# A four-layer graph network on one core: input rows loaded by ScalarE's queue, index rows turned amid the table, and shares of the node stages given to GpSimd

## The chip, the cores and the metric

One Trainium2 chip, one core. The time is the device time of one execution in microseconds (us), as a median of three runs. PE is TensorE, DVE is VectorE, ACT is ScalarE, POOL is GpSimd, SP is SyncE.

## The reference

Four graph layers over the same graph of 6250 nodes with 128 features and 100000 edges, sorted by destination. Each layer takes h = relu(layernorm(x)) and adds its result to x:

```python
h = relu(layernorm(x)); x = x + gat(h)      # 8 heads, softmax over the edges of a node and its own loop, batch norm
h = relu(layernorm(x)); x = x + gcn(h)      # sum over edges, scaled by the roots of both degrees, a product, batch norm
h = relu(layernorm(x)); x = x + pna(h)      # mean, deviation, minimum and maximum over edges, 13 parts times W, batch norm
h = relu(layernorm(x)); x = x + gatv2(h)    # leaky relu of x_l[src] + x_r[dst], a dot product, softmax, weighted sum
```

The GATv2 layer ends with `relu(out / denominator + bias)`, which is added to x and stored.

## The kernel before

The nodes stand in 49 tiles of 128 rows; `X` holds all of x in SBUF (128 partitions x 49 tiles x 128). The edges stand in 832 steps of 128, eight steps to a group, 104 groups. The program is a chain of blocks; between two blocks all engines meet. There are ten of them:

1. `build_steps`: loads x and the weights, counts how many edge chunks belong to each step, gathers the edges of each step from DRAM, makes index rows from them, and at the same time makes the first node table (layer norm, a transpose, a product with W: `rows_of`, `turn_rows`, `project`).
2. `gat_pass`, names beginning with `e_`.
3. `gat_to_gcn`, names `f0_` and `r0_` (printed `f_` and `r_`).
4. `sum_pass`, `s_`. 5. `gcn_to_pna`. 6. `moments_pass`, `m_`.
7. `pna_to_gatv2`, names `f2_` and `r2_` (printed `f_` and `r_`).
8. `gatv2_pass`, `v_`, and the end of `layer_gatv2`.

A pass (`gat_pass`, `sum_pass`, `moments_pass`, `gatv2_pass`) begins with POOL gathering the source rows of one step at a time from the node table in DRAM by an indirect DMA (`gather_step`, line 856, or L1749), into a ring of group buffers `G`. The other engines turn each group into sums per destination tile, which DVE adds into `ACC`. Before the first addition `ACC` is set to zero, once per pass.

A node stage (`gat_to_gcn`, `gcn_to_pna`, `pna_to_gatv2`) goes over the 49 tiles in chunks of four (13 chunks) or, in `pna_to_gatv2`, of three (17 chunks). Its second half is written with the class `ResidualNorm`, whose steps for chunk j are: `apply` (ACT, batch norm and relu on columns), `back` (PE, transposes back to rows), `add` (DVE, X += result), `statistics` (DVE, mean and variance of each row), `row_root` (POOL, 1/sqrt as a power), `shift` (DVE, nmr = -mean/deviation), `normalise` (ACT, H = relu(X*rstd + nmr)), `turn` (PE), `turned_in` (ACT copy from PSUM to `HT`), and a product on PE. In `pna_to_gatv2` the order of PE in round j is `back(j)`, `turn(j - 2)`, product(j - 3), and both bias rows are added by DVE when it takes the products out of PSUM (L2616 and L2618).

The order of the work on every engine is that of the written loops: nothing is reordered by a scheduler. Waits are counts of semaphores. In `build_steps`, PE first counts chunks (L616, L620), then turns and projects the table chunk by chunk (L628, L635), and turns the index rows at its end (L658); DVE takes those out of PSUM (L602 to L606). The last block's end is short:

```python
for t in range(tl.start, tl.stop):
    ins = V.scalar_tensor_tensor(ACC[:, t, 1:D + 1], ACC[:, t, 1:D + 1], rd[:, t:t + 1], g["bias3"][:], ALU.mult, ALU.add)
...
V.scalar_tensor_tensor(g["X"][:, tl, :], ACC[:, tl, 1:D + 1], 0.0, g["X"][:, tl, :], ALU.max, ALU.add)
```

## Time and profile before

| | us |
|---|---|
| median of 3 runs | 4756.52 (4754.43 to 4757.53) |
| the profiled execution | 4756.6 |
| its span in the profile | 4754.8 |
| `build_steps` | 0 to 82.3 |
| `gat_pass` | 82.3 to 1165.4 |
| `gat_to_gcn` | 1165.8 to 1259 |
| `sum_pass` | 1259 to 2250 |
| `gcn_to_pna` | 2250 to 2329 |
| `moments_pass` | 2329 to 3390 |
| `pna_to_gatv2` | 3390 to 3643.6 |
| `gatv2_pass` | 3643.6 to 4728.5 |
| the rest of `layer_gatv2` | 4728.5 to 4754.8 |

The times of the stages are read off the timeline: a stage begins with the first instruction of its block. The profile shows one execution; it names for each instruction the idle time of its engine ahead of it and what ended that time. Since each block waits for the one before it, a stage that is shortened by a microsecond shortens the whole by one, unless its last engine is held by something else.

### The profile page before, as it was taken

The numbers are of one execution on the slowest core, as the hardware profiler recorded it, in microseconds if no ns is written. First come the engines' busy times: TensorE is split into PE (matmuls) and PEld (weight loads), VectorE is DVE, ScalarE is ACT, GpSimd is POOL, SyncE is SP. The second block draws the span as 40 slices with busy tenths as digits, with TensorE's granted clock in tenths as the row PEclk, the third lists the DMA queues.
The fourth block names the chain that finished last, engine by engine and source line by source line (L and its number), as shares of the span: only waits on it lengthen the run. The fifth ranks groups of instructions, "written<-read, shape, count | busy, mean of one in ns | idle before, by whom it ended". The sixth has DMA issues, their size and how long they took to land. (4 is left out here: it accounts for less than half of the span.)

```text
span 4754.8 us, 95466 instructions
## 1 busy us (share of the span) xinstructions
PE 3336.3 (70%) x21401; PEld 2878.0 (61%) x21402; DVE 3192.4 (67%) x8183; ACT 2417.6 (51%) x5426; POOL 3323.1 (70%) x3505
## 2 busy tenths in 40 slices
PE   3888888887533333334577777777696888888886
PEld 2666666666533333333476676767564777777775
DVE  5888888888533333334677777787656676666767
ACT  3666666665300000000577777777535666666664
POOL 4777777775677777776677777777524777777774
PEclk7555555555755566655799999899897888888887
DMA  7333333332122121111366666666422333333332
GB/s 131 88 84 86 86 84 86 86 86 54 49 52 53 53 53 53 53 53 44 120 184 184 185 185 185 181 186 183 145 63 50 76 79 80 80 80 80 79 78 72
DMA packets 367220, 462.19 MB, mean 97 GB/s; under 512 B 104067, under 2 KB 271235, under 8 KB 367104
## 3 DMA queue, kind: packets, MB, share of 16 engines
q0 software_dynamic: 107648, 226.35, 20.4%
q1 hardware_dynamic: 254176, 233.02, 16.3%
q10 hardware_dynamic: 5280, 1.58, 0.1%
q8 instruction: 36, 0.59, 0.1%
q14 instruction: 80, 0.66, 0.0%
HBM read 327.40 MB, written 134.06 MB: 97 GB/s over the span
## 5 line engine op out<-in xcount | busy, mean ns | idle before, releaser
L856 POOL DMA_INDIRECT e_G<-dr_tab,src_idx x832 | 810.3, 974 | 266.6 <-issue 253.2
L856 POOL DMA_INDIRECT m_G<-dr_tab,src_idx x832 | 798.2, 959 | 262.7 <-issue 246.4
L856 POOL DMA_INDIRECT v_G<-dr_tab,src_idx x832 | 791.5, 951 | 264.5 <-issue 248.3
L1749 POOL DMA_INDIRECT s_G<-dr_tab,chunk_src x784 | 740.0, 944 | 241.9 <-issue 238.6
L1837 PE MATMUL s_OUT<-s_G,s_S 128*128 x1664 | 380.2, 421 | 586.1 <-SPq L1781 578.4
L1837 PEld LDWEIGHTS s_OUT<-s_G,s_S 128*128 128x128 f32 x1664 | 354.7, 324 | 611.4 <-issue 611.4
L1793 DVE TENSOR_TENSOR ACC<-ACC,s_OUT 128x129 f32 x832 | 241.3, 290 | 604.5 <-PE s_OUT L1837 500.8
L1261 PE MATMUL e_OUT<-e_RH,e_S 128*128 128x144 f32 x1664 | 512.4, 476 | 2.4 <-DVE e_RH L1147 2.4
L2277 ACT COPY f_AT<-r_TP 128x512 f32<-128x512 f32 (+1 forms) x13 | 7.2, 555 | 973.6 <-PE r_TP L2299 973.6
L1994 DVE TENSOR_TENSOR ACC<-ACC,m_OUT 128x256 f32 x832 | 347.3, 417 | 222.3 <-PE m_OUT L2077 126.2
L1261 PEld LDWEIGHTS e_OUT<-e_RH,e_S 128*128 128x128 f32 x1664 | 405.3, 327 | 35.8 <-DVE e_RH L1147 18.4
L2076 PE MATMUL m_OUT<-m_G,m_S 128*128 128x128 f32 x1664 | 344.5, 290 | 41.2 <-DVE ACC L1994 39.1
L1567 DVE SCALAR_TENSOR_TENSOR ACC<-ACC,v_R,v_OUT 128x129 f32 x832 | 287.2, 345 | 83.3 <-issue 0.8
L2077 PE MATMUL m_OUT<-m_SQ,m_S 128*128 128x128 f32 x1664 | 332.1, 282 | 0.0
L1957 ACT COPY m_XB<-m_BK 128x512 f32<-128x512 f32 x416 | 226.8, 587 | 204.6 <-PE m_BK L2060 201.6
L1658 PE MATMUL v_OUT<-v_RH,v_S 128*128 128x129 f32 x1664 | 311.1, 343 | 0.8 <-DVE ACC L1567 0.8
L1173 DVE TENSOR_TENSOR ACC<-ACC,e_OUT 128x144 f32 x832 | 252.8, 304 | 83.4 <-PE e_OUT L1261 0.4
L2051 PE MATMUL m_GT<-eye,m_G 128*128 128x128 f32 x832 | 133.4, 312 | 249.1 <-DMA m_G<-dr_tab,src_idx 196.5
L2076 PEld LDWEIGHTS m_OUT<-m_G,m_S 128*128 128x128 f32 x1664 | 265.4, 201 | 65.3 <-DVE ACC L1994 58.4
L1447 ACT COPY v_NXS<-v_NX 128x512 f32<-128x512 f32 x208 | 120.4, 579 | 310.9 <-PE v_NX L1611 304.2
L1658 PEld LDWEIGHTS v_OUT<-v_RH,v_S 128*128 128x128 f32 x1664 | 264.6, 241 | 18.2 <-ACT v_RH L1462 10.8
L1021 ACT ACTIVATE e_APART<-iota_row,e_LOC 128x128 bf16<-128x128 f32 x832 | 264.1, 388 | 19.4 <-ACT e_LOC L1017 19.1
(380 smaller groups left out, 8123.9 us busy)
## 6 DMA issues: line engine op xcount, KB each, us to landing
dr_ends<-m_XB SPq DMA_DIRECT2D x416, 256.0 KB, 3.2
e_LR<-dr_row_loc SPq DMA_DIRECT2D x104, 256.0 KB
m_MS<-dr_row_start SPq DMA_DIRECT2D x104, 256.0 KB
v_LR<-dr_row_loc SPq DMA_DIRECT2D x104, 256.0 KB
e_G<-dr_tab,src_idx POOLq DMA_INDIRECT x832
m_G<-dr_tab,src_idx POOLq DMA_INDIRECT x832
v_G<-dr_tab,src_idx POOLq DMA_INDIRECT x832
s_G<-dr_tab,chunk_src POOLq DMA_INDIRECT x784, 2.5
```

The lines of the kernel that those rows point to most:

```text
L856: pool.indirect_dma_start(out=out, out_offset=None, in_=table, in_offset=bass.IndirectOffsetOnAxis(ap=g["src_idx"][:, step:step + 1], axis ...
L1021: ins = nc.scalar.activation(APART[:, s, :], g["iota_row"][:], ACT.Square, bias=LOC[:, b, s:s + 1], scale=-1.0)
L1173: V.tensor_tensor(dst, dst, OUT[:, s // 3, (s % 3) * AC:(s % 3 + 1) * AC], ALU.add).then_inc(acc_done, 1)
L1261: nc.tensor.matmul(OUT[:, s // 3, (s % 3) * AC:(s % 3 + 1) * AC], S[:, b % 2, s, :], RH[:, b % 2, s, :], start=True, stop=True).then_inc(m ...
L1567: V.scalar_tensor_tensor(dst, dst, R[:, b % 2, s:s + 1], OUT[:, s // 3, (s % 3) * AC:(s % 3 + 1) * AC], ALU.mult, ALU.add).then_inc(acc_do ...
L1658: nc.tensor.matmul(OUT[:, s // 3, (s % 3) * AC:(s % 3 + 1) * AC], S[:, b % 2, s, :], RH[:, s, :], start=True, stop=True).then_inc(mm_done, 1)
L1749: pool.indirect_dma_start(out=G[:, c % (RING * GROUP), 0:D], out_offset=None, in_=table[:, :], in_offset=bass.IndirectOffsetOnAxis(ap=g["c ...
L1793: V.tensor_tensor(dst, dst, OUT[:, b, s // PER, (s % PER) * AC:(s % PER + 1) * AC], ALU.add).then_inc(acc_done, 1)
L1837: ins = nc.tensor.matmul(OUT[:, b, s // PER, (s % PER) * AC:(s % PER + 1) * AC], S[:, b, s, :], G[:, bass.ds(slot, 1), :].rearrange("p o c ...
L1994: V.tensor_tensor(dst, dst, OUT[:, q % 3, (s % 2) * 2 * D:(s % 2 + 1) * 2 * D], ALU.add).then_inc(acc_done, 1)
L2076: nc.tensor.matmul(OUT[:, q % 3, lo:lo + D], S[:, c, s, :], G[:, b, s, :], start=True, stop=True)
L2077: ins = nc.tensor.matmul(OUT[:, q % 3, lo + D:lo + 2 * D], S[:, c, s, :], SQ[:, c, s, :], start=True, stop=True)
```

## The change

In `build_steps`, the loads of x leave SP's queue and stand in ACT's queue, ahead of the nineteen weight loads. POOL's roots of the first four sets of rows stand ahead of the gathers of the edges. DVE's statistics of the first rows stand earlier. PE counts the chunks after the first product instead of at the start, and turns edges, locations and chunk numbers during the table (rounds 10 to 13); at the end only the `loc_end` rows are turned.

```diff
+                for i in range(EARLY):
+                    root(i)
...
-                whole_tiles = (TILES - 1) * P
-                rows = x[0:whole_tiles, :].rearrange("(t p) d -> p t d", p=P)
-                for c in range(4):
-                    piece = slice(c * XCN * CN, (c + 1) * XCN * CN)
-                    sp.dma_start(g["X"][:, piece, :], rows[:, piece, :]).then_inc(x_in[c], 16)
-                sp.dma_start(g["X"][0:LAST, TILES - 1, :], x[whole_tiles:N, :]).then_inc(x_in[4], 16)
...
+                whole_tiles = (TILES - 1) * P
+                rows = x[0:whole_tiles, :].rearrange("(t p) d -> p t d", p=P)
+                for c in range(4):
+                    piece = slice(c * XCN * CN, (c + 1) * XCN * CN)
+                    act.dma_start(g["X"][:, piece, :], rows[:, piece, :]).then_inc(x_in[c], 16)
+                act.wait_ge(setup, 12)
+                act.dma_start(g["X"][0:LAST, TILES - 1, :], x[whole_tiles:N, :]).then_inc(x_in[4], 16)
...
+                row_statistics(0)
+                row_statistics(1)
+                row_shift(0)
...
+                for k in range(IT):
+                    dve.wait_ge(edges_turned, k + 1)
+                    wide = slice(k * P, min((k + 1) * P, PICKED))
+                    V.tensor_copy(g["src_idx"][:, cols(k)], ps_c[:, k % 2, P:2 * P])
+                    V.tensor_scalar(g["loc"][:, cols(k)], ps_c[:, k % 2, 0:P], -1.0, None, ALU.add)
+                    V.tensor_copy(g["chunk_src"][:, wide], ps_c[:, k % 2, 2 * P:2 * P + wide.stop - wide.start]).then_inc(edges_taken, 1)
...
-                    cols = slice(k * P, (k + 1) * P)
-                    V.tensor_scalar(g["loc"][:, cols], ps_t[:, k % 2, 0:P], -1.0, None, ALU.add)
-                    V.tensor_scalar(g["loc_end"][:, cols], ps_t[:, k % 2, P:2 * P], -1.0, None, ALU.add)
-                    wide = slice(k * P, min((k + 1) * P, PICKED))
-                    V.tensor_copy(g["src_idx"][:, cols], ps_t[:, k % 2, 2 * P:3 * P])
-                    ins = V.tensor_copy(g["chunk_src"][:, wide], ps_t[:, k % 2, 3 * P:3 * P + wide.stop - wide.start])
-                    then(ins)
-
+                    dve.wait_ge(ends_turned, k + 1)
+                    V.tensor_scalar(g["loc_end"][:, cols(k)], ps_c[:, k % 2, 3 * P:4 * P], -1.0, None, ALU.add).then_inc(ends_taken, 1)
...
+                    if j == 1:
+                        count_chunks()
+                    if 10 <= j < 14:
+                        if j == 10:
+                            pe.wait_ge(v_done, 13)
+                            pe.wait_ge(readied, 4)
+                        for k in range(2 * (j - 10), min(2 * (j - 9), IT)):
+                            turn_edges(k)
```

In `gat_pass` and in `moments_pass`, the setting of `ACC` to zero is taken from DVE and given to ACT, as a copy with scale 0. After its last gather in `gat_pass`, POOL adds and scales the attention logits of the nodes' own loops.

```diff
+                pool.tensor_tensor(own_slope, own_slope, destination, ALU.add).then_inc(own_logits, 1)
+                pool.wait_ge(own_logits, 1)
+                pool.tensor_scalar(destination, own_slope, SLOPE, 0.0, ALU.mult, ALU.add).then_inc(own_logits, 1)
+                pool.wait_ge(own_logits, 2)
...
+                nc.scalar.activation(ACC[:].rearrange("p t c -> p (t c)"), g["ones"][:, 0:1].to_broadcast([P, TILES * AC]), ACT.Copy,
+                                     scale=0.0).then_inc(acc_done, 1)
...
-                V.memset(ACC[:], 0.0).then_inc(acc_done, 1)
...
+                nc.scalar.activation(ACC[:].rearrange("p t c -> p (t c)"), g["ones"][:, 0:1].to_broadcast([P, TILES * 2 * D]), ACT.Copy,
+                                     scale=0.0).then_inc(acc_done, 1)
...
-                V.memset(ACC[:], 0.0).then_inc(acc_done, 1)
```

In `gat_to_gcn`, DVE's chain has two steps fewer, the scaling of the nodes' own rows (`XPA`) is POOL's, and so are five of the thirteen scalings of table rows (chunks 1, 3, 6, 8, 11, the list `on_pool`).

```diff
+        self.on_pool = [j for j in range(self.n) if j % 5 in (1, 3)]
...
+                pool.wait_ge(chain, CHAIN)
+                for j in range(st.n):
+                    by_head(pool, XPA, es, j, own_scaled)
...
+                        if j - 2 in st.on_pool:
+                            scale_rows(pool, j - 2, st.pool_taken)
...
-                c.then(V.tensor_tensor(es[:], XPA[:, :, D:D + HEADS], XPA[:, :, D + HEADS:], ALU.add))
-                c.then(V.tensor_scalar(mx[:], es[:], SLOPE, None, ALU.mult))
-                c.then(V.tensor_tensor(es[:], es[:], mx[:], ALU.max))
-                c.then(V.tensor_tensor(mx[:], r[:], es[:], ALU.max))
+                c.then(V.tensor_tensor(es, es, XPA[:, :, D + HEADS:], ALU.max))
...
-                        by_head(ACC, r, j, rows_scaled)
-                        by_head(XPA, es, j, own_scaled)
+                        by_head(V, ACC, r, j, rows_scaled)
```

In the last phase of `pna_to_gatv2`, POOL makes H without the relu (`normalise_rows`, three tiles a chunk, after `row_root` of the next chunk), ACT applies the relu when it copies the transposed rows, the bias of the second product comes from a matmul with one row of ones ahead of it, and ACT instead of DVE takes that product to `XR`.

```diff
+    def normalise_rows(self, pool, j):
+
+        pool.wait_ge(self.nmr_done, j + 1)
+        wait(pool, self.turned, j - self.R + 1)
+        for u in range(self.width(j)):
+            t = j * self.ch + u
+            ins = pool.tensor_scalar(self.H[:, j % self.R, u, :], self.g["X"][:, t, :], self.rstd[:, t:t + 1], self.nmr[:, t:t + 1],
+                                     ALU.mult, ALU.add)
+        ins.then_inc(self.h_done, 1)
...
+        func = ACT.Copy
         if out is None:
             wait(act, self.product, j - 1)
-            out = self.HT[:, j % 2, 0:self.width(j), :]
-        self.nc.scalar.copy(out, self.TP[:, j % 2, 0:self.width(j) * P].rearrange("p (u n) -> p u n", n=P)).then_inc(self.ht_in, 1)
+            out, func = self.HT[:, j % 2, 0:self.width(j), :], ACT.Relu
+        self.nc.scalar.activation(out, self.TP[:, j % 2, 0:self.width(j) * P].rearrange("p (u n) -> p u n", n=P), func).then_inc(self.ht_in, 1)
...
-                    st.row_root(pool, j)
+                for j in range(st.n + 1):
+                    if j < st.n:
+                        st.row_root(pool, j)
+                    if j >= 1:
+                        st.normalise_rows(pool, j - 1)
...
-                    if 0 <= j - 2 < st.n:
-                        st.normalise(act, j - 2)
-                    if j >= 3:
+                    if 0 <= j - 3 < st.n:
                         st.turned_in(act, j - 3)
+                    i = j - 4
+                    if i >= 0:
+                        act.wait_ge(st.product, i + 1)
+                        nc.scalar.activation(XR[:, st.tiles(i), :], OP[:, 2 * (i % 2) + 1, 0:st.width(i) * D].rearrange("p (u d) -> p u d", d=D),
+                                             ACT.Copy, scale=-1.0).then_inc(xr_in, 1)
...
-                            ins = nc.tensor.matmul(OP[:, 2 * (i % 2) + 1, u * D:(u + 1) * D], st.HT[:, i % 2, u, :],
-                                                   g["W3"][:, D + 1:2 * D + 1], start=True, stop=True)
+                            own = OP[:, 2 * (i % 2) + 1, u * D:(u + 1) * D]
+                            nc.tensor.matmul(own, g["ones"][0:1, :], g["b3"][0:1, D + 1:2 * D + 1], start=True, stop=False)
+                            ins = nc.tensor.matmul(own, st.HT[:, i % 2, u, :], g["W3"][:, D + 1:2 * D + 1], start=False, stop=True)
...
-                                        per_feature(g["b3"][:, 0:D + 1], w), ALU.add)
-                        V.scalar_tensor_tensor(XR[:, st.tiles(i), :], OP[:, 2 * (i % 2) + 1, 0:w * D].rearrange("p (u d) -> p u d", d=D), -1.0,
-                                               per_feature(g["b3"][:, D + 1:2 * D + 1], w), ALU.mult, ALU.subtract).then_inc(st.taken, 1)
+                                        per_feature(g["b3"][:, 0:D + 1], w), ALU.add).then_inc(st.taken, 1)
```

At the end of `layer_gatv2`, DVE does the chunks 0 to 6 as before. For the chunks 7 to 12 ACT scales and rectifies, and POOL adds the bias and adds to X.

```diff
-                for j in range(NCH):
+                for j in range(HERE):
...
+                for j in range(HERE, NCH):
+                    for t in range(j * CH, min((j + 1) * CH, TILES)):
+                        ins = nc.scalar.activation(ACC[:, t, 1:D + 1], ACC[:, t, 1:D + 1], ACT.Copy, scale=rd[:, t:t + 1])
+                    ins.then_inc(scaled, 1)
+                    if j > HERE:
+                        rectify(j - 1)
+                rectify(NCH - 1)
...
+                def add(j):
+                    tl = slice(j * CH, min((j + 1) * CH, TILES))
+                    pool.wait_ge(rectified, j - HERE + 1)
+                    pool.tensor_tensor(g["X"][:, tl, :], g["X"][:, tl, :], ACC[:, tl, 1:D + 1], ALU.add).then_inc(other_rows, 1)
+
+                for j in range(HERE, NCH):
+                    tl = slice(j * CH, min((j + 1) * CH, TILES))
+                    pool.wait_ge(scaled, j - HERE + 1)
+                    pool.tensor_tensor(ACC[:, tl, 1:D + 1], ACC[:, tl, 1:D + 1], per_feature(g["bias3"][:], tl.stop - tl.start), ALU.add).then_inc(biased, 1)
+                    if j > HERE:
+                        add(j - 1)
+                add(NCH - 1)
...
```

Three places as they stand in the built programs, one row for each run of equal instructions. The first is PE's beginning in `build_steps`, where `before` holds the comparison of edge numbers that is counted, `ps_t`, `ps_c`, `ps_p` and `ps_o` are PSUM, and H is a chunk of normalised rows. Before:

```order
L616 MATMUL ps_c<-before,ones_bf 128x448 x14
L620 MATMUL ps_p<-ones_bf,before 128x1 x49
L641 MATMUL ps_t<-eye,W 128x128
L644 MATMUL ps_t<-AB,WT 128x16
L628 MATMUL ps_c<-eye,H 128x128 x6
L635 MATMUL ps_p<-W,HT 128x144 x3
L628 MATMUL ps_c<-eye,H 128x128 x3
L635 MATMUL ps_o<-W,HT 128x144 x3
```

And now, where the counting (`before`) has moved behind two turns and one product:

```order
L666 MATMUL ps_t<-eye,W 128x128
L669 MATMUL ps_t<-AB,WT 128x16
L653 MATMUL ps_t<-eye,H 128x128 x6
L660 MATMUL ps_p<-W,HT 128x144 x3
L641 MATMUL ps_c<-before,ones_bf 128x448 x14
L645 MATMUL ps_n<-ones_bf,before 128x1 x49
L653 MATMUL ps_t<-eye,H 128x128 x3
L660 MATMUL ps_o<-W,HT 128x144 x3
```

The 14 counting matmuls of 448 columns and the 49 of one column have moved from the head of PE's program to behind its first product; nothing else changes place in these rows.

The second is DVE at the start of `moments_pass`, where `m_XT` and `m_zero` are small work tiles. Before:

```order
L1996 MEMSET m_XT 128x1
L1997 MEMSET m_XT 128x1
L1998 MEMSET m_zero 128x256
L1999 MEMSET ACC 128x12544
L2005 CAST m_all_ones<-ones 128x128
L2006 TENSOR_SCALAR m_not_later<-iota_row,iota_col 128x128
```

And now, with the setting of `ACC` gone from DVE:

```order
L2064 MEMSET m_XT 128x1
L2065 MEMSET m_XT 128x1
L2066 MEMSET m_zero 128x256
L2072 CAST m_all_ones<-ones 128x128
L2073 TENSOR_SCALAR m_not_later<-iota_row,iota_col 128x128
```

DVE's later rows have moved up by one, into the place of the removed one.

The same place on ACT, where `m_MN`, `m_LOC` and `m_APART` are the first masks. Before:

```order
L1939 UNCONDITIONAL_BRANCH
L1945 ACTIVATE m_MN<-m_MS 128x1024 x2
L1960 COPY m_LOC<-loc 128x8
L1964 ACTIVATE m_APART<-iota_row,m_LOC 128x128 x8
L1968 ACTIVATE m_S<-m_APART,ones 128x1024
```

And now, with `ACC` ahead of the masks:

```order
L2005 UNCONDITIONAL_BRANCH
L2042 ACTIVATE ACC<-ones 128x12544
L2011 ACTIVATE m_MN<-m_MS 128x1024 x2
L2026 COPY m_LOC<-loc 128x8
L2030 ACTIVATE m_APART<-iota_row,m_LOC 128x128 x8
L2034 ACTIVATE m_S<-m_APART,ones 128x1024
```

ACT's masks have moved back by one instruction of 12544 elements.

The third is the last phase of `pna_to_gatv2` on POOL, where `r_mv` holds means and variances and `r_rstd` the roots. Before:

```order
L798 TENSOR_SCALAR r_rstd<-r_mv 128x3
L800 TENSOR_TENSOR r_rstd<-r_rstd,mhalf 128x3
L798 TENSOR_SCALAR r_rstd<-r_mv 128x3
L800 TENSOR_TENSOR r_rstd<-r_rstd,mhalf 128x3
L798 TENSOR_SCALAR r_rstd<-r_mv 128x3
```

And now, where three tiles of H stand behind each pair of root instructions:

```order
L838 TENSOR_SCALAR r_rstd<-r_mv 128x3
L840 TENSOR_TENSOR r_rstd<-r_rstd,mhalf 128x3
L868 TENSOR_SCALAR r_H<-X,r_rstd,r_nmr 128x128 x3
L838 TENSOR_SCALAR r_rstd<-r_mv 128x3
L840 TENSOR_TENSOR r_rstd<-r_rstd,mhalf 128x3
L868 TENSOR_SCALAR r_H<-X,r_rstd,r_nmr 128x128 x3
```

POOL's next pair of root instructions has moved behind three instructions of 128 elements.

And on PE, one round of it. Before:

```order
L772 MATMUL r_TB<-eye,r_UT 128x128 x3
L828 MATMUL r_TP<-eye,r_H 128x128 x3
L2534 MATMUL f_OP<-W,r_HT 128x129
L2536 MATMUL f_OP<-W,r_HT 128x128
L2534 MATMUL f_OP<-W,r_HT 128x129
L2536 MATMUL f_OP<-W,r_HT 128x128
L2534 MATMUL f_OP<-W,r_HT 128x129
L2536 MATMUL f_OP<-W,r_HT 128x128
```

And now, with one more matmul for each tile, from `b` and `ones`:

```order
L812 MATMUL r_TB<-eye,r_UT 128x128 x3
L886 MATMUL r_TP<-eye,r_H 128x128 x3
L2617 MATMUL f_OP<-W,r_HT 128x129
L2620 MATMUL f_OP<-b,ones 128x128
L2621 MATMUL f_OP<-W,r_HT 128x128
L2617 MATMUL f_OP<-W,r_HT 128x129
L2620 MATMUL f_OP<-b,ones 128x128
L2621 MATMUL f_OP<-W,r_HT 128x128
L2617 MATMUL f_OP<-W,r_HT 128x129
L2620 MATMUL f_OP<-b,ones 128x128
L2621 MATMUL f_OP<-W,r_HT 128x128
```

The order of the turns and products is the same; a product of a chunk has nine matmuls in place of six.

## Rows read from the trace of the kernel before

**Rows 1.** the head of the page

```profile
span 4754.8 us, 95466 instructions
...
PE 3336.3 (70%) x21401; PEld 2878.0 (61%) x21402; DVE 3192.4 (67%) x8183; ACT 2417.6 (51%) x5426; POOL 3323.1 (70%) x3505
```

**Rows 2.** the page's groups of instructions, count, then busy us and mean ns, idle

```profile
L856 POOL DMA_INDIRECT m_G<-dr_tab,src_idx x832 | 798.2, 959 | 262.7 <-issue 246.4
...
L1957 ACT COPY m_XB<-m_BK 128x512 f32<-128x512 f32 x416 | 226.8, 587 | 204.6 <-PE m_BK L2060 201.6
```

**Rows 3.** the timeline of build_steps: start, length, instruction, [idle before <- its end]

```profile
14.60 8.38 SPq L397 DMA_DIRECT2D X<-in_x_dram  x4
...
15.75 1.28 ACT L449 ACT_TABLE_LOAD   x1 [15.75 <-issue]
...
25.32 1.37 PE L620 MATMUL ps_p<-ones_bf,before 128*128 128x1 bf16 x49
...
38.85 2.42 ACT L435 ACTIVATE H<-X,nmr,rstd 128x128 f32<-128x128 f32 x6 [5.28 <-DVE nmr L499]
...
39.00 1.12 DVE L550 CAST ef<-edges 128x1792 f32<-128x1792 int32 x1 [0.19 <-DMA edges<-dr_step_rows,chunk_i]
...
57.16 0.17 DVE L571 TENSOR_TENSOR carried<-key,kprev 128x7 f32<-128x7 f32 x1 [2.25 <-DMA knext<-dr_keys]
...
71.61 1.09 DVE L597 TENSOR_TENSOR key<-locp,v 128x896 f32<-128x896 f32 x1
```

**Rows 4.** one line, L602: count, durations, first and last start

```profile
L602 DVE TENSOR_SCALAR loc<-ps_t x7: 290/291/292, 75.5 to 81.0; 128x128 f32<-128x128 f32 x7
```

**Rows 5.** the timeline of gat_pass's start

```profile
88.59 7.68 POOL L856 DMA_INDIRECT e_G<-dr_tab,src_idx  x1 [0.30 <-issue]
...
89.04 5.94 DVE L1075 MEMSET ACC<- 128x7056 f32 x1 [1.54 <-issue]
```

**Rows 6.** what DVE's first step of a group, L1096, waited for: us, times

```profile
  DMA e_G<-dr_tab,src_idx: 3.0, 3
```

**Rows 7.** the timeline of moments_pass's start

```profile
2329.87 13.89 POOL L856 DMA_INDIRECT m_G<-dr_tab,src_idx  x1 [9.55 <-POOLq L2243]
...
2332.24 10.51 DVE L1999 MEMSET ACC<- 128x12544 f32 x1 [2.56 <-issue]
...
2354.11 1.06 ACT L1950 ACTIVATE m_SQ<-m_G 128x1024 f32<-128x1024 f32 x1 [13.94 <-DMA m_G<-dr_tab,src_idx]
```

**Rows 8.** the timeline of sum_pass's start

```profile
1260.04 5.33 DVE L1797 MEMSET ACC<- 128x6321 f32 x1 [1.25 <-issue]
1260.47 0.96 POOL L1749 DMA_INDIRECT s_G<-dr_tab,chunk_src  x1 [0.31 <-issue]
```

**Rows 9.** the timeline of gat_to_gcn, a chunk of its second half

```profile
1223.04 1.27 POOL L822 TENSOR_TENSOR X<-X,r_H 128x512 f32<-128x512 f32 x1
...
1223.76 0.57 DVE L804 SCALAR_TENSOR_TENSOR r_nmr<-r_mv,r_rstd 128x4 f32<-128x4 f32 x1
```

**Rows 10.** the timeline of pna_to_gatv2, a chunk of its last phase

```profile
3605.50 0.39 PE L2534 MATMUL f_OP<-W,r_HT 128*128 128x129 f32 x2
...
3605.72 0.39 PE L2536 MATMUL f_OP<-W,r_HT 128*128 128x128 f32 x2
...
3606.07 0.85 POOL L800 TENSOR_TENSOR r_rstd<-r_rstd,mhalf 128x3 f32<-128x3 f32 x1
```

**Rows 11.** one line, L781, in that phase

```profile
L781 DVE TENSOR_TENSOR X<-r_TB,X x12: 292/552/558, 3604.1 to 3633.5; 128x384 f32<-128x384 f32 x11, 128x128 f32<-128x128 f32 x1
```

**Rows 12.** two DVE lines of the end of layer_gatv2

```profile
L2671 DVE SCALAR_TENSOR_TENSOR ACC<-ACC,rd,bias 128x128 f32<-128x128 f32 x49 | 13.9, 344 | 0.0
L2674 DVE SCALAR_TENSOR_TENSOR X<-ACC,X 128x512 f32<-128x512 f32 (+1 forms) x13 | 8.6, 661 | 0.4
```

**Rows 13.** POOL's timeline at the start, operations of 128 elements and more

```profile
1.80 0.19 POOL L348 MEMSET X<- 128x128 f32 x1
...
3.33 0.78 POOL L353 TENSOR_SCALAR_AFFINE_SELECT eye<-eye 128x128 f32<-128x128 f32 x1 [0.17 <-POOL intp L351]
```

More of the change, by code:

```diff
@@ L361, in _ @@
                         in_offset=bass.IndirectOffsetOnAxis(ap=chunk_i[:, k:k + 1], axis=0)).then_inc(gathered, 16)
[L363 to L368 removed]
+                for i in range(EARLY, NRT):
+                    root(i)
             @block.sync
@@ L811, in normalise @@
             wait(act, self.xh_done, j - self.R + 1)
-        wait(act, self.turned if self.TP is not None else self.taken, j - self.R + 1)
+        if self.TP is not None:
+            wait(act, self.turned, j - self.R + 1)
+        elif j >= self.R:
+            act.wait_ge(*self.row_taken(j - self.R))
         for u in range(self.width(j)):
@@ L822, in add_rows, with row_taken @@
         pool.tensor_tensor(X, X, self.H[:, j % self.R, 0:self.width(j), :], ALU.add).then_inc(self.xh_done, 1)
+    def row_taken(self, j):
+        here = [i for i in range(j + 1) if (i in self.on_pool) == (j in self.on_pool)]
+        return (self.pool_taken if j in self.on_pool else self.taken), len(here)
     def turn(self, pe, j):
@@ L863, in onehot_rows, with gat_pass @@
             loc[:, bass.ds(k * GROUP, GROUP)].unsqueeze(2).to_broadcast([P, GROUP, P]))
-def gat_pass(nc, g, table, destination, ACC, lo_f, hi_f):
+def gat_pass(nc, g, table, XPA, ACC, lo_f, hi_f):
     heads, hd, AC = HEADS, HF, ACC.shape[2]
+    own_slope, destination = XPA[:, :, D:D + heads], XPA[:, :, D + heads:D + 2 * heads]
     WC = D + heads
@@ L2631, in layer_gat @@
         ACC = ctx.enter_context(nc.sbuf_tensor("ACC0", [P, TILES, D + 2 * HEADS], F32))
-        gat_pass(nc, g, g["tab0"], XPA[:, :, D + HEADS:D + 2 * HEADS], ACC, lo_f, hi_f)
+        gat_pass(nc, g, g["tab0"], XPA, ACC, lo_f, hi_f)
         gat_to_gcn(nc, g, ACC, XPA, H0)
@@ L2679, in _, with store @@
                 rows = out[0:whole, :].rearrange("(t p) d -> p t d", p=P)
-                for j in range(NCH - 1):
+                def store(j):
+                    sp.dma_start(rows[:, j * CH:(j + 1) * CH, :], g["X"][:, j * CH:(j + 1) * CH, :]).then_inc(stored, 16)
+                for j in range(HERE):
                     sp.wait_ge(out_rows, j + 1)
-                    sp.dma_start(rows[:, j * CH:(j + 1) * CH, :], g["X"][:, j * CH:(j + 1) * CH, :]).then_inc(stored, 16)
-                sp.wait_ge(out_rows, NCH)
+                    store(j)
+                    if 2 <= j < 2 + NCH - 1 - HERE:
+                        sp.wait_ge(other_rows, j - 1)
+                        store(HERE + j - 2)
+                sp.wait_ge(other_rows, NCH - HERE)
                 sp.dma_start(out[whole:N, :], g["X"][0:LAST, TILES - 1, :]).then_inc(stored, 16)
```

206 lines of the change are left out of this document (122 added, 84 removed).

## The prediction

> **What bounds the kernel now.** The head of the page says that no engine is busy for more than about 70% of the span [rows 1], so an average tells nothing of this change: it touches six stages with six different limits. I read each stage in the timeline and asked which wait ends last there.
>
> In the passes POOL issues the gathers, one after the other. In moments_pass a gather takes 0.96 us on average and as much again as 0.3 goes by before the next [rows 2]; 832 of them fill the pass (798.2 busy and 262.7 idle make 1061 us, which is the pass). So whatever delays its first gathers delays the pass. The reader is to see that the first gather took 13.89 us [rows 7]. It overlaps DVE's memset of ACC, 10.51 us long. In gat_pass the fourth gather took 7.68 us, and beside it lies the memset of 7056 elements, 5.94 us [rows 5]. In sum_pass a memset of 6321 elements lies beside gathers of 0.96 us that are not delayed [rows 8]; that stage keeps its memset. So the delay belongs to these two memsets and not to every one.
>
> In the two node stages and in the tail DVE, PE and ACT share chains in which POOL had time to spare; the tail is DVE alone, 49 operations of 0.28 and 13 of 0.6 in pitch, 22.0 us from 4729.3 to 4751.2 [rows 12].
>
> **The change part by part.** Signs: minus is faster.
>
> *Moments pass.* The memset leaves DVE. Without it the first gather is an ordinary one. It had begun 2.37 us before the memset began (2332.24 - 2329.87), though, and I don't see what held it in that time. If nothing else holds it, 13.89 - 0.96 = 12.9 is saved; if the 2.37 stay, 10.5. I take 11.5. ACT sets ACC to zero instead: by its copy of 512 elements, 0.587 us [rows 2], 12544 elements are at most 14 us and, without the fixed part, some 11.7. ACT starts at 2329.9 and would be done at 2341.6, followed by masks of 6 us. ACT waited 13.94 us for the first group's landing at 2354.11 [rows 7]; that landing moves to about 2342, so ACT is some 6 us late with its first squares, and catches up during the second group's gathers, which take 10. If that cover were gone, 6 us of the 11.5 would be lost. Term: **-11.5** (-12.9 to -5.5).
>
> *Gat pass.* The same move saves 7.68 - 0.94 = 6.7 us of POOL. But this pass isn't gather-bound: in its whole length DVE's first step of a group waits for a gather three times, 3.0 us in all [rows 6]. More than that can't be won, since other loads end the rest of the wait at the start. ACT's 7056 elements (6.6 us) lie in time in which ACT waits for its first rows. POOL's two operations of 392 elements stand behind the last gather and are read only by the next stage; at 2.5 ns an element (below) they are 1.5 us, and the pass goes on 16 us longer. Term: **-2.3** (-3.0 to 0).
>
> *Build stage.* ACT's queue first: its 22 loads end at 15.75 [rows 3]; the five loads of x, 2.1 us each by SP's four in 8.38, come ahead, so its computing starts at 26.2, and after the table load of 1.28 the first rows come at about 28.2, not 38.85. That is 10.6 us earlier for the table. PE counts only after two chunks are turned, 3.4 us later, at 31.6, and needs 5.7 (4.3 for the wide part, 1.37 for the last, which ended at 26.69 [rows 3]), so it is done at 37.3: 10.6 later. Behind it hang the gathers of the edges: their landing goes from 39.0 to 49.6, and the neighbours' keys from 57.16 to 67.8, or 67 since less statistics stands between. Then DVE has about seven operations of 896 elements at 1.09 [rows 3], 7.7 in all: 74.7. The index rows are mostly turned already; seven rounds of one operation are left, 0.35 each where rounds of four took (81.0 - 75.5) / 6 = 0.92 [rows 4]: 77.2. The last row store must land as well: 79, against 82.3. What is late next is the table: PE stands still at round 10 until the edges' locations are there (about 59), and seven rounds of 2.1 and their stores end at 79 too. Term: **-3.3** (-8 if counting or keys come 5 us earlier than I have it, to +2 if the loads of x or the stores queue longer).
>
> *gat_to_gcn.* The chain loses two operations, 1.0. POOL's scaling of XPA takes 1.27 us a chunk, since POOL's addition of the same size does [rows 9], where DVE needed 0.6. The same rows show more: DVE's small nmr, 0.13 elsewhere, took 0.57 and ended when POOL's addition ended. Two operations that both read two SBUF operands stand one behind the other. In the first half DVE's scaling and statistics (1.2) and POOL's 1.27 then leave 1.87 a chunk where PE sets 1.79: 13 x 0.08, and 0.7 at the start: +1.8. In the second half five chunks get 1.28 more on POOL, whose 2.94 a chunk was near the period of 3.3: +1.5. Term: **+2.3** (-1 to +6).
>
> *pna_to_gatv2.* The period was (3633.5 - 3604.1) / 11 = 2.67 [rows 11]. PE had room for no more: a product of six matmuls at 0.22 [rows 10] and two turnings are 2.0. Nine matmuls make it 2.68 with the turnings. Worse is the new chain: from the end of back(j - 1) there follow DVE's addition and statistics (1.6), POOL's root (0.2 + 0.85 and the handovers, 1.2), three tiles of H on POOL, and then PE's turn(j - 2) in round j. In between PE has back(j) and a product. Let L be the length of that chain; PE's cycle closes at P = (L + 2.68) / 2. A tile on POOL lies between the memset's 0.14 and the select's 0.78 [rows 13]; I take 0.3, nearer to the memset since both only stream one operand, so L = 3.86 and P = 3.27. With 0.14 it is 3.03, with 0.78 4.0. So 17 x 0.6 = 10, and the first three products at half the clock cost 1.3 each instead of 0.6: another 2. DVE's and ACT's trade of the XR operation is worth nothing, since neither sets P. Term: **+11** (+5 to +23).
>
> *Tail.* DVE's seven chunks take 12.4 us. ACT and POOL do six, POOL with two operations of 1.27 for five chunks and two small ones: 13.5, from 4731. Side by side this would end at 4744.8, 6.4 earlier. But DVE's operations here read ACC and the bias, or ACC and X, and POOL's too. If they stand one behind the other in full, it is 12.4 + 13.5 = 25.9 against 22.0: +3.9. If DVE's fixed parts (about half of each 0.28) overlap, it is 8.3 + 13.5 = 21.8, nothing. I take **+1.5** (-6.4 to +3.9).
>
> Sum: -11.5 - 2.3 - 3.3 + 2.3 + 11 + 1.5 = -2.3 us. The profiled execution took 4756.6, which is the median of 4756.52; so 4754.3, and I say 4754.
>
> **Two rules beside this.** The Trainium skill, SBUF — State Buffer, section on the two separate sides, says that DVE and GpSimd share one port pair as an exclusive lock, held for the whole instruction. By that rule, the trace agrees: 13.89 and 0.57. It would price the tail at +3.9 (rival C). The Trainium skill, GPSIMD Engine Reference, section 3.1, gives an operation of two operands on GpSimd about 2.6 cycles an element against one on DVE. The trace agrees with 1.27 against 0.6; it speaks against moving the two-operand work, and the sum by it is the same.
>
> **The rivals.** About 0.2% of this kernel, 9.5 us, can be told from no change.
>
> A, clearly faster (27%): POOL's work is cheap and doesn't contend. A tile of H costs 0.14, pna_to_gatv2 gives +5; the tail gains its 6.4; gat_to_gcn is even. Sum -12.9 - 2.3 - 3.3 + 0 + 5 - 6.4 = -19.9: 4737. For it speaks that POOL idles in all three stages; against it the 0.57.
>
> B, clearly slower (16%): one mechanism, POOL's tile of H. At 0.78 a tile P is 4.0, and the term is 17 x 1.33 + 2 = 24.6, 13.6 more than mine: 4768. It decides from 0.65 a tile on (P 3.8, +9.5 in all). For it: the row that computes takes 0.78; against: it does a comparison of indices.
>
> C, the change doesn't do what it says (10%): what holds the first gather isn't the memset, or ACT's late masks hold the first groups by as much; with that -11.5 becomes -3 and the tail +3.9: 4756.6 + 8.6 = 4765. For it: the 2.37 us before the memset.
>
> The forecast (47%): gains and losses cancel, 4747 to 4762.
>
> **How the numbers follow.** Forecast within 0.2% for nearly all of its 47%; of C half lies within and half above; A is faster and B slower but for some edges, and the terms' ranges put a few of the forecast's cases on either side. So faster 0.31, same 0.46, slower 0.23. The range that leaves out a tenth on either side, into A and into B: 4739 to 4768.
>
> **What would show it.** Moments pass: a first gather of 1 to 3.4 us, and the first squares some 11 us earlier. Gat pass: gathers all of 0.94 at the start, the pass shorter by under 3. Build stage: counting from 31.6, the block's end near 79. pna_to_gatv2: L781's starts 3.27 apart, PE waiting for H from POOL ahead of turn. Tail: DVE's operations between POOL's, longer than 0.34, and the last store near 4753. I'd be wrong if POOL's tiles of H cost 0.14 or 0.78, or if a pass doesn't move by its first gathers.

## The result, and the profile after

The changed kernel takes 4823.08 us (4818.24 to 4825.87, 4 runs) against 4757.02 us of the kernel before: ratio 1.0135, 95% interval 1.0121 to 1.0149. It is 66 us slower. The forecast was 4754 with a range of 4739 to 4768, so it was wrong, and by far more than any of its rivals.

The head of the page of the changed kernel, which answers to [rows 1], with the granted clock in 40 slices:

```profile
span 4821.5 us, 95682 instructions
...
PE 3404.0 (71%) x21499; PEld 2929.7 (61%) x21500; DVE 3168.6 (66%) x8117; ACT 2434.2 (50%) x5423; POOL 3362.4 (70%) x3586
...
PEclk8555555555756655556899999999985788888887
```

The same line of the kernel before:

```profile
PEclk7555555555755566655799999899897888888887
```

Each digit is the granted clock of one slice of about 120 us, in tenths. The tenth digit from the end is to be read: it is a 5 (3616 to 3737 us, the end of `pna_to_gatv2`) where the kernel before has a 7 (3566 to 3685 us).

Since each pass begins and ends with POOL's gathers, their first and last starts cut a run into stages. They are read from the views of the tiles `e_G`, `s_G`, `m_G` and `v_G`; the differences are:

| stretch | before | after | moved | forecast |
|---|---|---|---|---|
| start to first gather of gat_pass (build) | 83.0 | 90.9 | +7.9 | -3.3 |
| from there to the start of gat_to_gcn | 1082.8 | 1084.6 | +1.8 | -2.3 |
| gat_to_gcn, to the first gather of sum_pass | 93.3 | 95.0 | +1.7 | +2.3 |
| sum_pass and gcn_to_pna | 1070.8 | 1070.3 | -0.5 | 0 |
| moments_pass's gathers | 1050.5 | 1037.7 | -12.8 | -11.5 |
| from the last of them to gatv2_pass | 263.9 | 331.1 | **+67.2** | +11 |
| gatv2_pass and tail | 1110.5 | 1111.9 | +1.4 | +1.5 |

One stage holds the whole loss. Its timeline, one tile of the product in the last phase, answers to [rows 10]: start, length, instruction.

```profile
3641.14 1.31 POOL L868 TENSOR_SCALAR r_H<-X,r_rstd,r_nmr 128x128 f32<-128x128 f32 x3
...
3641.15 0.79 PE L2620 MATMUL f_OP<-b,ones 1*128 1x128 f32 x2
...
3641.87 0.80 PE L2621 MATMUL f_OP<-W,r_HT 128*128 128x128 f32 x2
...
3642.46 0.64 PE L2617 MATMUL f_OP<-W,r_HT 128*128 128x129 f32 x2
...
3643.03 0.79 PE L2620 MATMUL f_OP<-b,ones 1*128 1x128 f32 x2
```

A tile's bias matmul begins 1.88 us behind the last one's (3641.15 to 3643.03), and not 0.66 (three at 0.22). POOL's three tiles of H take 1.31 and are not what PE waits for: PE has no idle time in these rows. The weight loads of the same tile show where the time goes:

```profile
3641.15 0.50 PEld L2620 LDWEIGHTS f_OP<-b,ones 1*128 1x128 f32 x2 [0.23 <-issue]
...
3641.87 0.50 PEld L2621 LDWEIGHTS f_OP<-W,r_HT 128*128 128x128 f32 x2 [0.23 <-issue]
...
3642.25 0.55 PEld L2617 LDWEIGHTS f_OP<-W,r_HT 128*128 128x128 f32 x2
```

The weights of L2617 are loaded from 0.21 us ahead of its matmul (3642.25 and 3642.46). Those of the one-row matmul L2620 and of the full one behind it, L2621, begin only together with their matmuls. The windows of the phase:

```profile
3600.00:3630.00 30.00, 30.00 (x105) 23.88 (x104) 8.27 (x36) 6.30 (x12) 9.38 (x20) 0.50 0.09 27
3630.00:3690.00 60.00, 60.00 (x209) 48.21 (x209) 17.99 (x78) 13.36 (x26) 21.24 (x46) 0.50 0.11 30
```

In such a row stand the window, its length, then the busy time of PE, of its weight loads, DVE, ACT and POOL, then the granted clock and the share and rate of the DMAs. PE is busy for 60.00 of 60 us and is granted 0.50 of its clock, the lower of its two levels, 1.2 GHz, all the time. In the kernel before, the same phase begins at 0.50 and rises; there PE was busy for 4.13 of 6 us before the rise and was granted the upper level, 2.4 GHz, behind it:

```profile
3594.00:3600.00 6.00, 4.13 (x18) 3.63 (x19) 3.41 (x20) 5.05 (x12) 3.07 (x6) 0.50 0.01 3
3606.00:3612.00 6.00, 5.24 (x44) 4.65 (x43) 5.62 (x22) 5.12 (x13) 2.68 (x5) 1.00 0.24 67
```

The start of moments_pass in the changed kernel answers to [rows 7]; its first gather went as forecast:

```profile
2340.15 10.65 ACT L2042 ACTIVATE ACC<-ones 128x12544 f32<-128x12544 f32 x1 [5.88 <-PEq L2318]
...
2340.79 1.06 POOL L915 DMA_INDIRECT m_G<-dr_tab,src_idx  x1 [9.69 <-POOLq L2318]
...
2356.35 1.04 ACT L2016 ACTIVATE m_SQ<-m_G 128x1024 f32<-128x1024 f32 x1
```

The first gather takes 1.06 us, so the 2.37 us ahead of DVE's memset, which I could not explain, went with the memset too. The first squares come at 2356.35, 15.6 us after the first gather begins, where it was 24.2. That is 8.7 sooner and not the "some 11" of the prediction, since ACT is still at its masks when the rows are there.

The build stage answers to [rows 3]:

```profile
2.13 13.78 ACTq L444 DMA_DIRECT2D X<-in_x_dram  x4
...
18.63 2.59 ACTq L448 DMA_DIRECT2D WF<-in_L_gnn_W_post_dram  x1
...
32.00 1.28 ACT L467 ACT_TABLE_LOAD   x1 [32.00 <-issue]
...
34.39 2.42 ACT L453 ACTIVATE H<-X,nmr,rstd 128x128 f32<-128x128 f32 x6
...
39.00 4.11 PE L641 MATMUL ps_c<-before,ones_bf 128*128 128x448 bf16 x14
...
56.67 1.09 DVE L580 CAST ef<-edges 128x1792 f32<-128x1792 int32 x1 [3.58 <-DMA edges<-dr_step_rows,chunk_i]
```

ACT's four loads of x took 13.78 us to issue, not 8.38, the fifth load of x 2.66, the next weight load 2.59, and the table load came at 32.00. Counting began at 39.00.

In the tail (it answers to [rows 12]) DVE and POOL take turns:

```profile
4794.35 1.14 DVE L2758 SCALAR_TENSOR_TENSOR ACC<-ACC,rd,bias 128x128 f32<-128x128 f32 x4
...
4795.71 2.73 POOL L2789 TENSOR_TENSOR ACC<-ACC,bias 128x512 f32<-128x512 f32 x2 [30.99 <-ACT ACC L2773]
4796.14 4.83 DVE L2758 SCALAR_TENSOR_TENSOR ACC<-ACC,rd,bias 128x128 f32<-128x128 f32 x4
...
4808.07 2.20 DVE L2758 SCALAR_TENSOR_TENSOR ACC<-ACC,rd,bias 128x128 f32<-128x128 f32 x4
...
4810.92 1.13 DVE L2758 SCALAR_TENSOR_TENSOR ACC<-ACC,rd,bias 128x128 f32<-128x128 f32 x4
...
4817.38 0.43 SPq L2808 DMA_DIRECT2D out_dram<-X  x1
```

Four of DVE's scalings take 1.14 alone, 4.83 beside POOL's additions, and 1.13 again when POOL is done.

### The profile page after: what moved, and what is told of

It reads as the page before. It is cut to its first block and busy times, and to the rows that moved or that the text cites. A ratio compares the mean times of both kernels' runs of the same rounds, so it can differ in the third digit from the quotient of the medians.

```text
span 4821.5 us, 95682 instructions
## 1 busy us (share of the span) xinstructions
PE 3404.0 (71%) x21499; PEld 2929.7 (61%) x21500; DVE 3168.6 (66%) x8117; ACT 2434.2 (50%) x5423; POOL 3362.4 (70%) x3586
## 5 line engine op out<-in xcount | busy, mean ns | idle before, releaser
L915 POOL DMA_INDIRECT v_G<-dr_tab,src_idx x832 | 791.8, 952 | 263.9 <-issue 250.2
L915 POOL DMA_INDIRECT m_G<-dr_tab,src_idx x832 | 785.3, 944 | 262.8 <-issue 247.1
```

What stands on the lines that cost most here:

```text
L915: pool.indirect_dma_start(out=out, out_offset=None, in_=table, in_offset=bass.IndirectOffsetOnAxis(ap=g["src_idx"][:, step:step + 1], axis ...
```

## The experiments

**The stage undone (e1_old_pna_end).** `pna_to_gatv2` and its `turned_in` are those of before; all else is the changed kernel.

> The changed kernel with pna_to_gatv2 as before; all other parts stay changed. The table of stages puts +67 of the +66 us into this stage, between the last gather of moments_pass and the first of gatv2_pass (263.9 before, 331.1 after). If stages add up, the kernel takes 4756, and the stage 264. If a part of the loss came from state left by earlier stages (clock, semaphores, queues), the stage stays above 270 and the kernel above 4762.

Measured: 4754.98 us against 4759.08 of before, ratio 0.9991, interval 0.9981 to 1.0; the stage took 264.2. So the stages add up: the whole loss of 66 us sits in this stage, and the gains and losses of the others come to about -4.

**Without the one-row matmul (e2_no_bias_row).** POOL still makes H; DVE instead of ACT takes the product to `XR` again, with the bias. This run and the next two were done once each; the repeated runs of one kernel on this chip lie within 7 us of one another.

```diff
-                            nc.tensor.matmul(own, g["ones"][0:1, :], g["b3"][0:1, D + 1:2 * D + 1], start=True, stop=False)
-                            ins = nc.tensor.matmul(own, st.HT[:, i % 2, u, :], g["W3"][:, D + 1:2 * D + 1], start=False, stop=True)
+                            ins = nc.tensor.matmul(OP[:, 2 * (i % 2) + 1, u * D:(u + 1) * D], st.HT[:, i % 2, u, :],
+                                                   g["W3"][:, D + 1:2 * D + 1], start=True, stop=True)
```

> The changed kernel, but the bias of the second product is added by DVE as before (L2618) and no one-row matmul stands in front; H is still POOL's. Theory K (the one-row matmuls keep the granted clock at 0.50): the clock rises, and the chain through POOL sets the period: POOL's three tiles take 1.31, so L is 4.2, P = (4.2 + 2.0) / 2 = 3.1, the stage takes about 272 and the kernel 4764. Theory M (the gaps in which PE waits for POOL's H keep it low): the clock stays 0.50, P is (4.2 + 0.6 + 4.0) / 2 = 4.4, the stage takes about 292 and the kernel 4784.

Measured: 4772.62, the stage 274.5. That is theory K's side (272), and 18 us short of M's. The clock rises: it is 1.00 from 3614 to 3650, although PE is then busy for 24.57 of 36 us, and the tenth digit from the end is a 7 again:

```profile
PEclk8555555555765556665799998999897888888887
```

**A full bias matmul (e3_bias_128_rows).** The same count of matmuls, all rows filled.

```diff
-nc.tensor.matmul(own, g["ones"][0:1, :], g["b3"][0:1, D + 1:2 * D + 1], start=True, stop=False)
+nc.tensor.matmul(own, g["eye"][:], g["b3"][:, D + 1:2 * D + 1], start=True, stop=False)
```

> The changed kernel, but the bias matmul multiplies the 128x128 identity by the 128 rows of the bias in place of one row of ones by one row: the same 128 columns and the same count of matmuls, with all rows filled. Theory K: the clock rises to 1.0, P = (4.2 + 2.68) / 2 = 3.4, the stage takes 278 to 283, the kernel 4772. Theory M or mere work (nine matmuls for six): the stage stays at 331 and the kernel at 4823.

Measured: 4769.27, the stage 279.9, within K's 278 to 283. The windows of its phase, before the clock rises, while it rises and after:

```profile
3590.00:3596.00 6.00, 2.00 (x8) 1.60 (x9) 3.33 (x18) 1.08 (x2) 4.87 (x11) 0.50 0.00 0
3596.00:3602.00 6.00, 6.00 (x45) 6.00 (x44) 2.33 (x13) 1.95 (x4) 2.68 (x7) 0.79 0.00 0
3602.00:3632.00 30.00, 22.73 (x197) 21.44 (x195) 17.53 (x76) 13.23 (x26) 20.31 (x43) 1.00 0.21 60
```

Nine full matmuls a chunk are granted the full clock, with PE busy for 22.73 of 30 us. More work at less busy time: it is neither the count of matmuls nor idle time that held the clock down, but that one in three had one row.

**The one-row matmul alone (e4_bias_row_alone).** The kernel before with only the bias matmul and ACT's copy of XR; H stays with ACT.

> The kernel before with only the one-row bias matmul and ACT's copy of XR added; H stays ACT's. Theory K: the clock stays at 0.50 through the phase, PE sets a period of 6.9, the stage takes 325 to 332 and the kernel 4820. Theory M: the clock rises as before, PE sets 2.7 to 2.9, the stage takes about 268 and the kernel 4761.

Measured: 4822.76, the stage 330.6. The one-row matmul makes the whole loss with H still on ACT (ACT's copy of XR, the other half of this edit, stands in e3 too, where the clock rises). POOL's H costs 10.6 us where the clock is high (274.5 in e2 against 263.9) and nothing on top of the low clock.

```profile
3630.00:3690.00 60.00, 60.00 (x210) 48.20 (x209) 17.50 (x77) 22.49 (x52) 8.46 (x17) 0.50 0.10 30
```

**The two settings of ACC alone (e5_two_memsets_alone, and again as e5b).** These two, and all of e5 to e11, ran on a chip on which the kernel before took 6550. The passes are longer there (the gathers of the four took 1135.1 to 1783.6 us in e5 where they took 977.7 to 1062.6), the straight stages are not (the first gather at 81.9 and 83.0). Only differences on that chip are used, and there the stages more than the totals: the kernel before spreads from 6526 to 6564.

> The kernel before with only the two settings of ACC moved from DVE to ACT. Theory L (the even-sized memsets on DVE hold POOL's descriptors up): first gather of moments_pass 1.06, its gathers end 12.8 earlier; gat_pass 2.7 shorter; kernel 15.5 less, 4741. Rival: part of these gains in the changed kernel came from its other edits (own logits, other start), then less than 12 in all.

> The same kernel as e5_two_memsets_alone, which ran on a chip on which every turn of the loops in the passes took some 5 us more (6550 us for the kernel before). Where before takes 4757, theory L says 4741.5 (-12.8 and -2.7).

Measured: ratio 0.9988 (0.9975 to 1.0002) and 0.9981 (0.997 to 0.9992), the second 5 to 20 us less. By the medians it is 10.2 and 9.5 less, where 15.5 was expected. The gathers of moments_pass took 1282.2 and 1281.6 where three kernels with the memset on DVE took 1295.3 to 1296.3 there: -13.8, which agrees with theory L. gat_pass with its end took 1646.0 and 1645.6 against 1647.0 to 1647.8: 1 to 2 less, and not 2.7.

**The build stage alone (e6_build_alone).**

> The kernel before with only build_steps changed. If the stage table of the changed kernel is right, the first gather of gat_pass moves from 83.0 to 90.9 and the kernel takes 4764.

Measured: the first gather at 89.1, where the kernels with the old stage had 81.9 to 83.1: +6.6, the kernel, in one run, 6564.89 against 6550.02. The loss of this stage is its own.

**Counting first (e9_count_first).** The changed build stage, the counting at PE's start.

```diff
+                count_chunks()
                 pe.wait_ge(first_in, 16 * len(first_loads))
...
-                    if j == 1:
-                        count_chunks()
```

> The changed build_steps alone, but PE counts the chunks at its start as before (x still loaded by ACT's queue, index rows still turned amid the table). Theory C (the counting, put behind the table's first product, makes the stage later): counting starts when DVE has compared, at about 22.4 in place of 39.0, the edges land some 16 earlier, and the block ends some 10 earlier, near 80. Theory Q (the loads of x ahead of the weights on ACT's queue make the table late, first rows 34.4): the table of 17 chunks then ends at 34.4 + 17 x 2.0 = 69, so the end is set by the keys and stays near 80 too; if the table were the bound, the end would stay at 89 to 91.

Measured: the first gather at 75.1, 14 earlier than with the counting behind the first product, and 7 earlier than before the change.

```profile
22.19 5.41 PE L641 MATMUL ps_c<-before,ones_bf 128*128 128x448 bf16 x14 [22.19 <-DVE before L545]
...
41.23 1.09 DVE L580 CAST ef<-edges 128x1792 f32<-128x1792 int32 x1 [3.60 <-DMA edges<-dr_step_rows,chunk_i]
```

The edges are there at 41.23 in place of 56.67. Theory C holds, by more than I had expected. The table (Q) was not the bound: ACT took its last product out at 66.5, and DVE its last index row at 72.7. ACT's queue still begins its computing as late as in the changed kernel.

**gat_to_gcn alone (e7_gcn_stage_alone).**

> The kernel before with only the change to gat_to_gcn (own logits on POOL at the end of gat_pass, XPA scaled by POOL, five chunks' table rows scaled by POOL). In the changed kernel the time from the last gather of gat_pass to the first of sum_pass is 119.7 against 113.5. Theory X (exclusive turns of POOL and DVE on operations that read SBUF twice): the same +6 here, kernel 4763. Rival: it came with the later memset or the clock: then +2.

Measured: 6557.71 in one run against 6551.85, and from the block's start to the first gather 95.2, where kernels with the old stage took 93.7 to 95.4 on that chip. The +6 that I had read into it wasn't there: 4.5 of it belong to the end of gat_pass. The other runs with this changed stage took 93.0 to 95.1 (e1, e2, e3, e11, e13, e14), and those with the old one 93.3 in the kernel before and 94.0 in e4. No cost of this stage can be told from nothing.

**The gaining parts together (e8_combined).** The two settings of ACC, the shorter chain, and a tail in which ACT scales and DVE adds, with nothing on POOL:

```diff
+                    if j < HERE:
                         for t in range(tl.start, tl.stop):
...
+                    else:
+                        dve.wait_ge(scaled, j - HERE + 1)
+                        ins = V.tensor_tensor(ACC[:, tl, 1:D + 1], ACC[:, tl, 1:D + 1], per_feature(g["bias3"][:], tl.stop - tl.start), ALU.add)
```

> The kernel before with what should gain and nothing else: ACC set by ACT in gat_pass and moments_pass (-15.5), the logits of the own loops made by POOL after its last gather and the chain of gat_to_gcn two operations shorter (-1.0), no POOL share in any node stage, and at the end ACT scaling the rows of the chunks 1 to 12 while DVE adds the bias and adds to X, two operations of 0.6 a chunk in place of 1.78 (about -5). Sum -21.5: 4735. If DVE's gain in the tail is lost to a wait for ACT (1.26 a chunk), 1 us less.

Measured: ratio 0.9979 (0.9965 to 0.9994), 17.6 less by the medians, where 21.5 was expected.

**And with the counting first (e10_combined_count_first).**

> The combination of e8_combined, and the changed build_steps with the counting at PE's start (e9_count_first moved the first gather of gat_pass from 82 to 75.1). Terms: -7 build, -12.8 moments_pass, -2.7 gat_pass, -1 gat_to_gcn, -5 tail: 28.5 less than before, 4728 where before takes 4757. If part of the tail or of the build term isn't additive, less than 25.

Measured: 6521.28 against 6551.85, ratio 0.9953 (0.9935 to 0.9971), 30.6 us less, with 28.5 expected. It beats the kernel before; the changed kernel was not run on this chip. Its tail, by lines:

```profile
L2754 ACT ACTIVATE ACC<-ACC,rd 128x128 f32<-128x128 f32 x45 | 13.3, 388 | 5.4 <-DVE rd L2735 5.4
L2747 DVE SCALAR_TENSOR_TENSOR X<-ACC,X 128x512 f32<-128x512 f32 (+1 forms) x13 | 8.6, 661 | 0.5
L2744 DVE TENSOR_TENSOR ACC<-ACC,bias 128x512 f32<-128x512 f32 (+1 forms) x12 | 7.8, 650 | 0.0
```

DVE needs 8.6 + 7.8 us of busy time, and 1.1 for the first chunk that it still scales, for what took 13.9 + 8.6 [rows 12]. The tail takes 21.4 us from its first operation to the end, where it took 26.3.

**How many rows (e11_bias_32_rows, e13_bias_64_rows).** The bias divided by 32 or 64 and summed over as many rows.

> The changed kernel, but the bias comes from 32 rows of ones by 32 rows of bias / 32, in place of one row or 128. Theory K in a strict form (any matmul with few rows keeps the clock at 0.50): like one row, stage 331, kernel 4823. Theory K by filling (a quarter of the rows in every third matmul is enough with the six full ones of each chunk): the clock rises, stage 280, kernel 4770. One row in 128 stands against 32; I lean to the second with 55%.

> The changed kernel, the bias from 64 rows of ones by 64 rows of bias / 64. One and 32 rows left the granted clock at 0.50 for the whole phase (stages 331 and 338), 128 rows let it rise (280). If filling counts as a mean over matmuls, two full and one half-full could be enough: stage 280, on a chip where the gather loops are slow too. If only nearly full ones do, the stage stays at 331 to 338.

Measured: with 32 rows the stage took 337.8 (331.1 on the other chip for one row; DVE's additions of a chunk are 6.92 us apart in both), so no rise. With 64 rows, on a third chip on which the kernel before took 4756.05, it took 307.2: the clock does rise, but only after some 50 us of unbroken work. Until then its rounds are 6.92 apart too.

```profile
3596.00:3644.00 48.00, 48.00 (x168) 38.47 (x167) 12.76 (x58) 10.21 (x20) 16.43 (x35) 0.50 0.09 25
3650.00:3680.00 30.00, 28.88 (x174) 22.36 (x172) 11.66 (x50) 8.38 (x19) 14.20 (x31) 1.00 0.19 54
```

This falls between my two cases. It also separates two things: at the same pitch the clock rose with 64 rows within 50 us and did not with one row in the 109 us from 3600 to 3709, so the wider gaps alone don't hold it down. The row at the full clock shows a second cost: 28.88 us for 174 matmul passes, 0.166 each, where full matmuls took 22.73 / 197 = 0.115 with time to spare.

**Rising and falling (e14_one_row_from_chunk_8).** Full bias matmuls for chunks 0 to 7, one-row ones from chunk 8 on.

> The changed kernel, with the 128-row bias matmul for chunks 0 to 7, in which the clock rises, and the one-row matmul for chunks 8 to 16. Theory R (one-row matmuls only keep a low clock from rising): it stays at 1.0 after chunk 8, stage 280. Theory F (they also make it fall): nine chunks at 0.50 take some 6.9 in place of 3.4, part of them before it falls: stage 295 to 312.

Measured: the stage 307.4, theory F.

```profile
3608.00:3626.00 18.00, 14.85 (x132) 14.32 (x131) 9.61 (x42) 8.04 (x16) 11.55 (x24) 1.00 0.20 56
3626.00:3632.00 6.00, 4.42 (x27) 3.50 (x27) 2.88 (x14) 1.57 (x3) 4.72 (x10) 0.87 0.23 67
3632.00:3680.00 48.00, 48.00 (x165) 38.01 (x165) 10.84 (x44) 8.71 (x18) 11.93 (x26) 0.50 0.10 30
```

The clock was at 1.00 and fell in the window from 3626, in which PE was still busy for 4.42 of 6 us; it stayed at 0.50 although PE was then busy for 48.00 of 48. In windows of 1 us it is 1.00 up to 3630, 0.69 in the next and 0.50 from 3631. PE had waited 1.58 us for POOL's H up to 3628.88, but just as long up to 3621.76, where the clock did not fall. The timeline of PE shows the last full bias matmul and the first ones of one row:

```profile
3626.37 0.39 PE L2621 MATMUL f_OP<-b,eye 128*128 128x128 f32 x2
...
3629.58 0.48 PE L2623 MATMUL f_OP<-b,ones 1*128 1x128 f32 x2
...
3630.83 0.79 PE L2623 MATMUL f_OP<-b,ones 1*128 1x128 f32 x2
...
3632.71 0.79 PE L2623 MATMUL f_OP<-b,ones 1*128 1x128 f32 x2
```

The first starts at 3629.58; the next tile's, 1.25 behind it, already takes 0.79 as in the rows of the changed kernel, and from then on the tiles are 1.88 apart.

## Why the prediction was wrong, point by point

**pna_to_gatv2, forecast +11, measured +67.** The step that failed is "the first three products at half the clock cost 1.3 each instead of 0.6: another 2", that is, the assumption that the clock rises within the first chunks; in the kernel before it had risen by the second product, which starts at 3601.70. The arithmetic of P = (L + 2.68) / 2 was for 1.0, and no rival had a clock that stays low. With one-row matmuls the clock is 0.50 for all 17 chunks, and a product's nine matmuls take 5.64 (3 x 1.88) where nine at the pitch that the kernel before had at 0.50, 0.43, would take 3.9. These are two of its products before its clock rose:

```profile
3598.11 0.64 PE L2534 MATMUL f_OP<-W,r_HT 128*128 128x129 f32 x2
...
3598.54 0.64 PE L2536 MATMUL f_OP<-W,r_HT 128*128 128x128 f32 x2
```

So both show: half the clock (+2.5 a chunk with the turnings), and 1.8 us a chunk more because the one-row matmul and its two neighbours start 0.72, 0.59 and 0.57 apart and not 0.43. The period of 6.92, where 3.27 was forecast, is then PE's alone, and POOL's L, on which I spent the working, never came to bear. Where the clock does rise (e2, e3), the formula held: with the measured 1.31 for three tiles (I had 0.9) it gave 272 and 278 to 283, and 274.5 and 279.9 were measured. Two of its sums don't come out as written: the named parts of L are 1.6 + 1.2 + 0.9 = 3.7 and not 3.86, and 10 and 2 make 12, not 11. The 0.14 for POOL's memset is the distance of two starts; its row says 0.19 [rows 13]. None of these matters beside the 56 us. Rival B would have been decided by the price of a tile, 0.435; it lay between my bounds and below the 0.65 from which B decides.

**Build stage, forecast -3.3, measured +7.9.** Three terms of the sum were mis-sized and all one way. The issue of x on ACT's queue: 13.8 + 2.7 us and not 10.5, and a weight load behind it 2.6, so ACT's computing started at 32.0 and not 26.2. Counting followed at 39.0, not 31.6, and the edges at 56.7, not 49.6. Behind the keys, DVE's part began at 78.5 (67 forecast), because DVE's turned rows stand ahead of it and wait for PE: SP had issued the loads of the keys by 69.0, and DVE was at those rows from 71.6 on. e9 shows which decision costs: the counting's place is worth 14 us, and with it undone the stage gains 7. I had worked out that it comes 10.6 later and still given the stage a gain, because I counted on the shorter end to pay for it.

**moments_pass, forecast -11.5, measured -12.8.** Right, by the mechanism named; the bound of -12.9 was nearly reached, and ACT's lateness was hidden as forecast. The Trainium skill, SBUF — State Buffer, section on the two separate sides, has DVE and GpSimd share one port pair as an exclusive lock, as the prediction cites it. With that these agree: 13.89 with DVE's memset, 1.06 without. Which of DVE's operations take the lock, the runs decide: beside the memset of 6321 elements the gathers took 0.96 [rows 8].

**gat_pass, forecast -2.3, measured +1.8.** The start did gain: DVE's first step comes 25.2 after the block's first long memset and not 26.0. But the 103 periods after it took 1043.6 in place of 1040.5. The five other kernels with the changed pass on the fast chips took 1041.8 to 1043.5, the one with the old pass 1040.8. On the slow chip the two kinds differ by under 1. What makes each period up to 0.03 longer stays open; ACT's setting of ACC and POOL's own logits were not tried apart on a fast chip. The first gather was not 0.94 as forecast but 2.79.

**gat_to_gcn, forecast +2.3, measured +1.7.** The same stage took 93.0 to 95.2 in the other runs that have it and 93.3 to 95.4 in those with the old one, so the agreement shows nothing: the cost is between none and 2 us.

**Tail, forecast +1.5, measured +1.6:** from its first operation to the end 27.9 where it was 26.3. The number is right by luck. DVE's four scalings of 1.14 took 4.83 beside POOL, so the operations do wait for one another, as rival C had it; but DVE ended 22.7 us after its start, as before, so the sum was that of the prediction's middle case ("nothing") and not C's +3.9. What is left is the last store, for which the prediction had no term: SP issues it 1.1 us after DVE's end, since in its program the stores of chunks 6 and 11 come first (its twelve others end at 4817.33). Before, it was 0.03.

## What to carry to other kernels

Don't add a bias on TensorE by a matmul of one row to a chain of full ones that lives from the full clock: 49 of them cost 51 us more than the same with 128 rows (331.1 against 279.9). With all 128 rows filled it cost 5 (279.9 against 274.5, where DVE adds the bias). Either fill them or leave the bias with the engine that empties PSUM. When a step is moved behind another on one engine, follow everything that hangs on it first, and only then what the move was for. Setting a large buffer to zero on ACT instead of DVE was worth 12.8 us, more than the memset's own 10.51, in the pass whose bound is POOL's gathers, and 1 to 2 at most in gat_pass, where it isn't. It is worth a look at the trace first: the memset of sum_pass held nothing up.
